# A message-passing layer on one core: node-pair comparison ahead of the additions, even batch shares, bias and split of x in short pieces

## The reference

```python
msg  = relu(x[src] + edge_attr @ We + be)           # 200000 x 128
aggr = segment_sum(msg, dst, num_segments=N)         # 6250 x 128
h = (1.0 + eps) * x + aggr
h = relu(h @ W1 + b1) @ W2 + b2
mu, var = mean(h, axis=0), var(h, axis=0)
h = (h - mu) * rsqrt(var + BN_EPS) * gamma + beta
out = layernorm(x + relu(h) + x)                     # over the 128 features
```

## Time and profile before

| what | us |
|---|---|
| median of 3 runs | 1575.66 (1574.07 to 1578.65) |
| the profiled execution, its own time | 1577.36 |
| its span, first to last instruction | 1575.4 |
| TensorE busy | 1417.6 (90%) |
| ScalarE busy | 1259.9 (80%) |
| GpSimd busy | 1154.0 (73%) |
| VectorE busy | 891.4 (57%) |
| mean granted TensorE clock | 0.978 |

### The profile page before, as it was taken

One profiled execution on the slowest core, in us unless ns is written; L12 is line 12 of the kernel. 1 busy time (PEld: TensorE's weight loads), 2 busy tenths in 40 slices (PEclk: granted clock), 3 DMA queues, 4 the chain that ended last, 5 costly groups with the idle time before them and its releaser, 6 DMA issues.

```text
span 1575.4 us, 60398 instructions
## 1 busy us (share of the span) xinstructions
PE 1417.6 (90%) x23395; PEld 1094.2 (69%) x23395; DVE 891.4 (57%) x3166; ACT 1259.9 (80%) x3709; POOL 1154.0 (73%) x1193
## 2 busy tenths in 40 slices
PE   1399999999999999999999999999999899999875
PEld 1277777777777777777777777777777677777534
DVE  4775566555566655655555555554555556555336
ACT  0588888888888888888788788787888778888655
POOL 7677777777777777777777777777777777777732
PEclk9999999999999999999999999999999999999987
DMA  9544454455444455445444444444444444444412
GB/s 261 160 108 112 111 121 111 111 119 122 112 112 107 114 120 112 112 113 118 106 113 109 104 112 112 106 111 106 112 106 108 109 105 112 117 112 112 153 27 83
DMA packets 148468, 180.72 MB, mean 115 GB/s; under 512 B 41677, under 2 KB 128932, under 8 KB 147924
## 3 DMA queue, kind: packets, MB, share of 16 engines
q1 hardware_dynamic: 102489, 89.62, 24.4%
q0 software_dynamic: 37728, 77.31, 20.8%
q10 hardware_dynamic: 7963, 9.90, 2.1%
HBM read 170.09 MB, written 6.63 MB: 112 GB/s over the span
## 4 chain that ended last, share of the span: by engine, by line
PE 40%; POOL 34%; issue 12%; DMA 5%; DVE 4%; ACT 3%; SPq 0%; ACTq 0%; POOLq 0%; DVEq 0%
POOL xg L575 34%; PE ps L1341 14%; PE ps L1326 10%; PE ps L1280 7%; PE ps L1266 5%; DMA xg<-xb,idxb 3%; DMA iota_all<-in_x 2%; ACT hot L720 1%; PE ps L1307 1%; ACT msg L726 1%; PE ps L1287 1%; PE ps L1405 1%; PE ps L1395 1%; PE ps L1310 1%; DVE msg L948 1%
## 5 line engine op out<-in xcount | busy, mean ns | idle before, releaser
L575 POOL DMA_INDIRECT xg<-xb,idxb x1145 | 1105.0, 965 | 359.2 <-issue 338.9
L948 DVE TENSOR_TENSOR msg<-ps,xg 128x512 f32<-128x512 f32 x390 | 265.1, 688 | 356.1 <-DMA xg<-xb,idxb 237.4
L689 ACT ACTIVATE iota_all<-ps 128x384 bf16<-128x384 f32 x896 | 379.5, 483 | 39.1 <-PE ps L1326 34.1
L713 ACT ACTIVATE hot<-iota,rel 128x64 f32<-128x64 f32 x1560 | 391.5, 339 | 0.0
L1341 PE MATMUL ps<-iota_all,hot_all 128*128 128x128 bf16 x4032 | 258.8, 220 | 0.0
L1341 PE MATMUL ps<-iota_all 128*128 128x128 bf16 x4032 | 258.5, 220 | 0.0
L1341 PEld LDWEIGHTS ps<-iota_all,hot_all 128*128 128x128 bf16 x4032 | 226.0, 98 | 43.9 <-issue 21.9
L1341 PEld LDWEIGHTS ps<-iota_all 128*128 128x128 bf16 x4032 | 225.7, 98 | 43.3 <-issue 41.0
L726 ACT ACTIVATE msg<-msg 128x512 f32<-128x512 f32 x390 | 241.1, 618 | 18.2 <-DVE msg L948 17.9
L1266 PE MATMUL ps<-we,ea 64*128 64x128 f32 x3126 | 233.0, 289 | 18.3 <-DVE msg L948 17.8
L1280 PE MATMUL ps<-msg,hot 128*64 128x128 f32 x3120 | 222.5, 287 | 23.3 <-ACT msg L726 22.6
(11 more groups left out here) (136 smaller groups left out, 1089.3 us busy)
## 6 DMA issues: line engine op xcount, KB each, us to landing
ea<-in_eat SPq DMA_DIRECT2D x156, 320.0 KB
lowB<-lowD SPq DMA_DIRECT2D x128, 224.0 KB
xg<-xb,idxb POOLq DMA_INDIRECT x1145
accT<-in_xt ACTq DMA_DIRECT2D x1, 3125.0 KB, 14.1
x<-in_xt ACTq DMA_DIRECT2D x1, 3125.0 KB, 11.0
iota_all<-in_x ACTq DMA_DIRECT2D x1, 3080.0 KB, 28.8
out<-iota_all SPq DMA_DIRECT2D x5, 512.0 KB
xb<-iota_all SPq DMA_DIRECT2D x3, 784.0 KB, 10.4
```

The costliest lines, as they stand in the source:

```text
L575: pool.indirect_dma_start(out=xg[0:rows, slot, j, :], out_offset=None, in_=of, in_offset=bass.IndirectOffsetOnAxis(ap=index, axis=0)).then ...
L689: act.activation(rows3[:, t, :, :].rearrange("p a h -> p (a h)"), ps_rows(k * NTILE + t), ACT.Copy)\
L713: last = act.activation(hot[:, q % TURN, m, :], iota, ACT.Abs, bias=rel[:, t:t + 1], scale=-1.0)
L948: add = dve.tensor_tensor(both, lin_of(half), xg[:, g % RING, :, :].rearrange("p (b t) h -> p b (t h)", b=2), ALU.add)
```

## The change

**VectorE in the loop.** `pairs_of` stands right behind `ranks`, ahead of the step's two additions; before, it stood behind the additions to `accT`.

**ScalarE in the loop.** Where a step has both, `take` now goes ahead of `keep_slots`. `slotS` and `lowB` have three buffers in place of two, and the waits for an old buffer fall back by one batch.

**Shares.** Which visit has which pick comes from one formula over all batches. The same 128 groups have batches. Each batch's seven picks now fall 3, 2, 2 over its three visits; before, every second batch had 2, 3, 2. `join` and `keep_rows` follow. The PSUM bank of a pick is its running number modulo 3 throughout.

**The beginning.** `lift` and `remains` work on two blocks (256 columns) at a time, seven instructions where there was one of 1792 columns. `split_sources` works on all 1560 tiles; before, on the 390 that belong to batches or will.

```diff
-    SHARE = tuple((3, 2, 2) if k % 2 else (2, 3, 2) for k in range(NB))
+    PER, OVER = 10, 30
+    def visit_of(b, t):
+        return ((b + SKIP) * NTILE + t) * OVER // (PER * NTILE) - 3
+    def group_of(b):
+        return visit_of(b, NTILE - 1) + 3
...
-        slotS = sb("slotS", [P, 2, EDGES], f16)
+        slotS = sb("slotS", [P, 3, EDGES], f16)
-        lowB = sb("lowB", [P, 2, NPAIR * CAP], f16)
+        lowB = sb("lowB", [P, 3, NPAIR * CAP], f16)
...
-        NCOL = NB * ITERS * HALF
+        NCOL = LOOPED * GROUP
...
             def lift(q):
                 a, b = PIECES[q][0], sum(PIECES[q])
                 dve.wait_ge(s_xrow, 32)
-                dve.tensor_tensor(xrow[0:SUB, a:b, :], xrow[0:SUB, a:b, :],
-                                  beb[0:SUB, :].unsqueeze(1).to_broadcast([SUB, b - a, HID]), ALU.add).then_inc(s_lifted, 1)
+                for c, d in short(a, b):
+                    last = dve.tensor_tensor(xrow[0:SUB, c:d, :], xrow[0:SUB, c:d, :],
+                                             beb[0:SUB, :].unsqueeze(1).to_broadcast([SUB, d - c, HID]), ALU.add)
+                last.then_inc(s_lifted, 1)
...
             def remains(q, which):
-                dve.tensor_tensor(to, xrow[0:SUB, a:b, :], x3[0:SUB, a:b, which, :], ALU.subtract)\
-                   .then_inc(s_rest[which], 1)
+                for c, d in short(a, b):
+                    to = xrow[0:SUB, c:d, :] if which == 0 else x3[0:SUB, c:d, 2, :]
+                    last = dve.tensor_tensor(to, xrow[0:SUB, c:d, :], x3[0:SUB, c:d, which, :], ALU.subtract)
+                last.then_inc(s_rest[which], 1)
...
 # VectorE, iteration
-                    for j, k in phase(i, q, 3):
-                        ranks(j, k)
+                    for b in phase(i, q, 3):
+                        ranks(b)
+                    for b in phase(i, q, 4):
+                        pairs_of(b)
                     add_x(i, 2 * q, n)
...
-                    for j, k in phase(i, q, 4):
-                        pairs_of(j, k)
...
 # ScalarE, iteration
-                    for j, k in phase(i, q, 3):
-                        keep_slots(j, k)
-                    for j, k in ending(i, 2 * q - 1):
-                        take(j, k)
+                    for b in ending(i, 2 * q - 1):
+                        take(b)
+                    for b in phase(i, q, 3):
+                        keep_slots(b)
```

More of the change, by code:

```diff
@@ L60, in gine_layer_kernel @@
     STEPS = ROUND // 2
-    RING = ROUND // 2
+    RING = 15
     TURN = 3
@@ L102, in gine_layer_kernel, with set_of @@
     assert NPAIR == NTILE * PAIRS and CAP * PAIRS == P
[L103 to L121, removed]
+    def visit_of(b, t):
+        return ((b + SKIP) * NTILE + t) * OVER // (PER * NTILE) - 3
+    def group_of(b):
+        return visit_of(b, NTILE - 1) + 3
+    NBATCH = next(b for b in range(LOOPED) if group_of(b) > 383)
+    BATCH_OF = {group_of(b): b for b in range(NBATCH)}
+    VISIT = {}
+    for b in range(NBATCH):
+        for t in range(NTILE):
+            VISIT.setdefault(visit_of(b, t), []).append((b, t))
+    assert len(BATCH_OF) == NBATCH and visit_of(0, 0) // 2 - 4 >= -PRELUDE
+    def set_of(b):
+        return b % 2
     FAR = 8192.0
@@ L223, in gine_layer_kernel @@
         src_f = hot_all[:, 4224:4224 + (TBLK + 1) * P].rearrange("p (b e) -> p b e", e=P)
-        assert 512 + 2 * NCOL <= FULL + 1 and 2560 + (TBLK + 1) * P <= 4224 and 4224 + (TBLK + 1) * P <= N and 0 < TREST
-        assert all(g % 3 == 2 for g in SORTED) and ROUND % 3 == 0
+        assert 3 * NCOL <= N and 2560 + (TBLK + 1) * P <= 4224 and 4224 + (TBLK + 1) * P <= N and 0 < TREST
         SEL1 = NPAIR * 2 * CAP
@@ L380, in phase, with prior, at_step @@
-        def phase(i, q, ahead):
[L382 to L387, removed]
+            return i * ROUND + g in BATCH_OF
+        def prior(b):
+            return b - 2 if b >= 2 else None
+        def at_step(b, t):
+            return b * NTILE + t
@@ L403, in gathered, with parts @@
[L403 to L410, removed]
+            return [b for b, t in visit(i, v) if t == NTILE - 1]
+        def parts(i, v):
+            steps = visit(i, v)
+            cut = next((m for m, (b, t) in enumerate(steps) if t == 0 and m), len(steps))
+            return steps[:cut], steps[cut:]
@@ L412, in run, with by_pool, gathered @@
+        def by_pool(n):
+            return GROUP - HALF * (n in BATCH_OF)
+        def gathered(n):
+            return 16 * sum(by_pool(m) for m in range(n % RING, n + 1, RING))
         def run(eng, iteration):
@@ L587, in iteration @@
                             pool.wait_ge(s_xb[q], stores(q))
-                    if not isinstance(i, int) or i or g >= RING:
-                        wait_apart(pool, s_pre, i * ROUND + g - RING + 1)
-                    for j in range(by_pool(i, g)):
-                        gather(g % RING, j, P, idxb[h][:, at + j:at + j + 1], s_xg[g % RING], xb if biased else x)
+                    if n >= RING:
+                        wait_apart(pool, s_pre, n - RING + 1)
+                    for j in range(by_pool(n)):
+                        gather(n % RING, j, P, idxb[h][:, at + j:at + j + 1], s_xg[n % RING], xb if biased else x)
             run(pool, iteration)
@@ L1010, in select_edges, with short @@
                 for t in range(NTILE):
-                    last = dve.tensor_scalar(sel2[set_of(k)][:, t, :], slotS[:, set_of(k), :], nodes[:, t:t + 1], None, ALU.is_equal)
+                    last = dve.tensor_scalar(sel2[set_of(b)][:, t, :], slotS[:, b % 3, :], nodes[:, t:t + 1], None, ALU.is_equal)
                 last.then_inc(s_sel2, 1)
+            def short(a, b):
+                return [(c, min(c + 2, b)) for c in range(a, b, 2)]
             def lift(q):
@@ L1378, in iteration @@
                         second_product(EARLY - 1, 0)
-                    for j, k, t in visit(i, 2 * q + 1):
-                        pick(j, k, t)
-                    for j, k, t in visit(i, 2 * q):
-                        join(j, k, t)
-                    for j, k in phase(i, q, 4):
-                        count(j, k)
+                    for b, t in visit(i, 2 * q + 1):
+                        pick(b, t)
+                    for b, t in new:
+                        join(b, t)
+                    for b, t in parts(i, 2 * q)[0]:
+                        join(b, t)
+                    for b in phase(i, q, 4):
+                        count(b)
                     if closing(i, q) and q == CLOSE:
```

263 lines of the change are left out of this document (118 added, 145 removed).

## The result

| what | before | after |
|---|---|---|
| median, us | 1576.35 (1574.07 to 1579.00, 13 runs) | 1580.06 (1577.38 to 1582.74, 13 runs) |
| ratio | | 1.0023, interval 1.0014 to 1.0031 |
| the profiled execution, its own time, us | 1577.36 | 1579.14 |
| its span, us | 1575.4 | 1577.0 |
| the 46th gather starts, us | 79.70 | 84.48 |

The change costs 0.23%, some 3.6 us, and in the two profiled executions only the beginning has become longer. The 46th gather is the first that needs a place in the ring again (15 groups of four gathers, five of them with three less, are 45). It comes 4.78 us later; from it on, the run takes no longer than before, and a gather of the loop takes 0.960 us on average (0.961 before). Single executions scatter: in the 14 traces of this case that stretch takes 1431.7 to 1437.3 us.

The account below looks back on a forecast made before the run. GpSimd's back-to-back gathers bound the kernel, their start set by VectorE's chain. Pieces 2.59 plus comparison 0.16 gave +2.75 us, on the median 1575.66 + 2.75 = 1578.4 us; own range 1574 to 1583, overall 1569 to 1586.

Parts of the forecast that it names:

- The price of a piece: Bias and remainders at the start: 256-column instructions start 0.341 us apart, so seven in place of one cost 0.43 us more.
- The bias's +0.43: VectorE's chain at the start: cutting the bias adds 0.43 us, since SP starts storing behind its first piece.
- The addition of group 0: VectorE's addition that the 46th gather waits for: later by 2.59 us from pieces and 0.16 us from the comparison ahead.
- short pieces should let it in sooner: GpSimd's gathers beside VectorE's pieces at the start: about 3.3 us saved beside the bias, 4.1 beside the second remainders.
- what is late next is the addition of group 0, as before: At the start: the 46th gather still waits for VectorE's addition of group 0, its wait growing beyond 3.27 us.
- no wait at the 46th gather: Sign against the forecast: the first gather needing a ring place again, expected near 82.5 us, would not wait for an addition.
- Freed gathers count nothing: At the start: time saved on gathers beside pieces counts as nothing, as waits of 7.61 and 3.27 us follow.
- The split of the sources: VectorE at the start: 1560 columns instead of 390 cost +4.2 us, covered by its 4.49 us wait for x.
- The consumers: Rival, 9%: ScalarE's order and two comparisons add 0.96 us a round, beyond the 0.70 reserve; consumers bound, 1587 to 1595 us.
- GpSimd's pace: Gathers over the whole run: 0.953 against 0.963 us between stretches, giving some 4 us of uncertainty either way.
- the rival of a faster GpSimd: Rival, 16%: VectorE slows fewer gathers in the loop, or gathers freed at the start count in full; 1568 or 1569 us.
- The supposition: Gathers beside VectorE instructions with two SBUF inputs: descriptors are not held up, so pieces would free nothing.

## Why the prediction was right, and which of its steps were not

The forecast was 1578.4 us, within 0.3% of before and 2.75 us slower on the chain; measured was a ratio of 1.0023, 3.6 us by it, and a median of 1580.06 in the range. Of the 1.7 us between the medians 0.7 is the kernel before, whose median over 13 runs is 1576.35. The mechanism is the one that it named: pieces make VectorE's chain longer, and the start waits for the chain. That the sum came out so near is in part luck, since one of its terms was not there and the held gather was not in it.

- **The price of a piece** held. 28 second remainders took 9.49 us, 0.336 from start to start (0.341 expected); against 7.83 for four whole ones this is +1.66 of the +1.73 forecast. Alone they moved the start by 2.0. The last one ended at 66.09 us, with 66.6 expected. (The upper bound of a piece, +0.93, is +0.92 by its own terms.)
- **The bias's +0.43** was not there: alone in pieces it moved the start by -0.02 us. The first piece came later, and SP's first store with it (in that kernel 2.46 us after the bias's start instead of 2.05), but its four stores then took 11.19 us instead of 11.83, so that the first gather from `xb` began 20.0 us after the bias's start in both. The stores scatter by more than the term: 10.92 to 11.83 us in the six traces with a whole bias, 10.86 to 11.23 in the eight with pieces. The first remainders alone moved the end of the second remainders by 0.52 (0.43 expected) and the start by 1.2; the rest is scatter of a single execution.
- **The addition of group 0** came 3.1 us later, with 2.59 + 0.16 expected. In the five traces with everything in pieces it is 2.2 to 3.1, 2.6 on average.
- **The step that failed** is "short pieces should let it in sooner" for the second remainders, and with it "what is late next is the addition of group 0, as before". It held beside the bias (1.04 us) and in the kernel with second remainders alone (1.04). In the changed kernel one gather stood still for 12.18 us instead, so the 46th had no wait that grew: GpSimd itself came late, at 84.48 and not near 82.5. The prediction had listed "no wait at the 46th gather" as a sign against it, and it was one: 1.6 us of the start here, up to 2.4 in two of the other kernels with everything in pieces.
- **Freed gathers count nothing** was right: a wait of 7.65 us took their place, then one of 15.09 where five more gathers had gone ahead of the wait for `xb`, while VectorE's chain was in front.
- **The split of the sources** took 6.65 us on VectorE (27.34 to 33.99) where it had taken 2.24, +4.4 with +4.2 expected, and stayed under the wait for x, of which 0.49 us is left.
- **The consumers** never became the bound; the loop's orders cost nothing. The rival's price was too high, 0.96 us a round against 0.44 measured, all of it ScalarE's: with the comparison back the consumers' round is 21.60 us, as in the changed kernel.
- **GpSimd's pace** did not change; the rival of a faster GpSimd falls with 0.960 us a gather. The two paces that the prediction took its 4 us of uncertainty from, 0.953 and 0.963, differ by how many gathers a window cuts: after the change 151.85 us of busy time are counted as 159 gathers in one window and as 158 in another.
- **The supposition** of the Trainium skill, "SBUF — State Buffer", section "Who interferes with whom", that such VectorE instructions would not hold up descriptors, is contradicted by these runs as by the rows before: a gather takes 1.63 us beside whole instructions, 1.04 beside pieces and 12.18 in the hold, against 0.94 alone. That they hold off GpSimd's reads, as the same section of the Trainium skill says, is not contradicted, since a gather reads its row numbers from `idxb` in SBUF; no run here tells the two apart. The 58 cycles of the Trainium skill, "VectorE: DVE Perf Modes", section on the TRN2 errata, agree for a row of pieces: 0.327 us estimated by them, 0.336 measured.

## What to carry to other kernels

Cutting an instruction into pieces has a fixed price on the engine that runs it (here 1.66 us for 24 more instructions in a row), and what it gives another engine counts only if that engine isn't waiting for this very chain: look at the next wait of the engine that is to gain. So free the chain first, then cut where the neighbour has work to do; in that order the same edit that gave nothing gave 1.5 us of the start. A slower consumer behind a bound producer shows up as less waiting for data, not as time, until the reserve is used up; doubling one cost tells how much is left.

## What the runs showed of the hardware that was not expected

An indirect gather on GpSimd that began after an idle time of GpSimd, while VectorE ran without a pause through instructions with two SBUF inputs, the last 28 of them 256 columns wide, ended only 0.8 us behind the last of these: it took 11.77 to 12.25 us, in five traces. In three others gathers beside pieces of 256 columns took 0.94 to 1.19 us. What decides between the two stays open.
